# Attention pooling over 512 rows: TensorE's small matmuls and VectorE's softmax grouped for two chunks at a time

## Chip, cores and metric

One core of one Trainium2 chip. The metric is device time in microseconds, the median of three executions of the whole kernel.

## The reference

```python
h = relu(einsum('bse,eh->bsh', behavior_emb, W_b) + (candidate_emb @ W_c)[:, None, :] + fc1_b)
scores = einsum('bsh,h->bs', h, fc2_w[:, 0]) + fc2_b[0]
attn = softmax(scores, axis=-1)
user_interest = einsum('bse,bs->be', behavior_emb, attn)
x = concatenate([user_interest, candidate_emb], axis=1)
z = relu(x @ mlp1_w + mlp1_b)
logit = (z @ mlp2_w + mlp2_b)[:, 0]
```

Here B = 512 rows, S = 200 positions, E = H = 128, and everything is f32. The behavior array (52.4 MB) is read twice: once as it stands (for the pooling) and once in a copy that is transposed on the host (for the first matmul), so that some 105 MB come in.

## The kernel before, in words

**Chunks and groups.** The 512 rows are cut into 32 chunks of 16 rows. A chunk has two loads of 1.6 MB: `xt` (transposed, for the hidden layer) and `x` (as it stands, for the weighted sum). Each has four buffers. A chunk's `xt` is treated in four groups g = 0 to 3 of 800 columns (32 partial rows of 25 positions).

**What is done for a group.** The hidden layer's matmul runs as three products of rounded halves. ScalarE makes the high half (`high_half`, L329, tile `xh`), VectorE the low half (`low_half`, L454, tile `xl` = xt - xh), TensorE adds hi x hi and hi x lo (L613, L614) and, when the low half is there, lo x hi (L617) into one of three two-bank PSUM tiles `z_ps` (`products`). Bias and ReLU are taken out of PSUM by VectorE for groups 0 and 2 (`biased_max`, L464) and by ScalarE for groups 1 and 3 (`biased_relu`, L371, four instructions). Which `z_ps` a group takes is a fixed rotation (`Z_SLOTS`); TensorE waits until that tile's last group has been read.

**What is done for a chunk.** `score` (L632) is 40 column-tiled matmuls, four 32-column tiles of the array side by side, that multiply the hidden layer by fc2. VectorE's `softmax` is six small dependent steps on one chunk's scores (L475 to L493); it ends with the bias of the exponent. ScalarE's `exponents` (L336) makes the weights, GpSimd's `mask_weights` (L299) spreads them over a block-diagonal tile, and `weighted_sum` (L643) is 56 column-tiled matmuls of these weights with `x`. Every second chunk ScalarE copies the sums out (`copy_pooled4`, L342), TensorE transposes them (`transpose_sums`, L684) and ScalarE copies the result to `pooled_t` (L346).

**Order.** Each engine's order is written out by hand in a `period(c, q, phase)`, one for each chunk c, q = c mod 4 (from L381 for ScalarE, L522 for VectorE, L754 for TensorE). TensorE's is: z of groups 0 and 1 of chunk c; one column-tiled stretch with the scores of chunk c-1 and then the weighted sum of chunk c-3 (LAG = 3); z of groups 2 and 3. VectorE's is:

```python
biased_max(c, 0); low_half(c, 3); softmax(c - 1)          # six steps
next_low(0); biased_max(c, 2); next_low(1); next_low(2)   # low halves of chunk c + 1
```

and ScalarE's: ReLU of group 1; high halves 0 and 1 of chunk c+1; (copy of the sums); exponents of chunk c-1; high half 2; ReLU of group 3; high half 3.

**Loads.** SyncE issues all large loads in one queue (L252 for `xt`, L260 for `x`), in the order xt(n), x(n-3), xt(n+1), x(n-2) and so on; the last five are xt(31), x(28), x(29), x(30), x(31). xt(n) waits until the low halves of chunk n-4 are made, x(n) until chunk n-4 is summed. The weights of the last layers (`later_sb`, L266) are loaded right behind x(0).

**End.** After z of group 3 of chunk 31 TensorE goes through: row sums of the weights of chunks 0 to 27; sum of 29; scores of 31; transpose; spreading of the inverses; sum of 30; one MLP product of the candidates; the second row sums; sum of 31; the second spreading; the other candidate products (L721); transpose of the last pair; the MLP products of the pooled rows (L727) for chunks 0 to 27 and for 28 to 31; the logits (L734). VectorE adds the output bias (L589) and SyncE stores the logits in two parts (L279).

## Time and profile before

| | |
|---|---|
| median of 3 runs | 266.76 us (266.63 to 266.91) |
| the profiled execution's own time | 266.47 us |
| its span | 264.7 us |
| TensorE busy | 259.3 us (98%) |
| VectorE busy | 224.2 us (85%) |
| ScalarE busy | 200.6 us (76%) |
| GpSimd busy | 29.4 us (11%) |
| HBM read | 105.63 MB, 399 GB/s over the span |

The span is what the trace covers; the execution's own time is 1.77 us longer. TensorE's matmuls overlap and their ends are modelled, so its busy share says little; the distances between the starts of instructions are what can be added up. All times in the rows are microseconds from the span's start. "[1.05 <-DMA xt...]" at a row's end is the idle time of the engine before that instruction and what ended it.

### The profile page before, as it was taken

The page shows a single profiled execution, that of the slowest core. Times are in us where ns is not written, and L with a number is a line of the kernel's source. Part 1 is how long each engine was busy: PE and PEld are TensorE (multiplying, and loading weights), DVE is VectorE, ACT ScalarE, POOL GpSimd, SP SyncE. Part 2 cuts the span into 40 slices and gives each one's busy share as a digit, 9 for nine tenths or more (in the row PEclk, how much of TensorE's full clock was granted, in tenths as well). Part 3 has the DMA queues.
Part 4 walks back from the last instruction along what each step waited for, and adds up shares of the span by engine and source line. Part 5 has one row for each costly group of instructions (what it writes and reads, how often), then busy time and mean ns, then how long its engine had stood idle before and what let it go on. Part 6 is the DMA issues. An engine that isn't in the chain of part 4 may idle for free.

```text
span 264.7 us, 10384 instructions
## 1 busy us (share of the span) xinstructions
PE 259.3 (98%) x3942; PEld 212.4 (80%) x3942; DVE 224.2 (85%) x397; ACT 200.6 (76%) x481; POOL 29.4 (11%) x38
## 2 busy tenths in 40 slices
PE   8999999999999999999999999999999999999995
PEld 7557788888888868888888888888888888888973
DVE  0479998999898988989899998989989898999541
ACT  2569888798887697878789887878888787889312
POOL 2003001111110111110111111011111100111100
PEclk9999999999999999999999999999999999999999
DMA  7999999999999999999999999999999999999900
GB/s 247 430 433 422 422 426 420 424 424 420 426 422 423 426 420 429 429 426 426 424 429 429 426 426 426 428 428 422 428 429 428 426 426 426 429 428 426 391 32 0
DMA packets 10544, 105.87 MB, mean 400 GB/s; under 512 B 1184, under 2 KB 1696, under 8 KB 2592
## 3 DMA queue, kind: packets, MB, share of 16 engines
q1 hardware_dynamic: 10240, 105.44, 94.7%
q8 instruction: 12, 0.20, 0.3%
q10 hardware_dynamic: 288, 0.20, 0.2%
q14 instruction: 4, 0.03, 0.0%
HBM read 105.63 MB, written 0.00 MB: 399 GB/s over the span
## 4 chain that ended last, share of the span: by engine, by line
PE 60%; DMA 18%; DVE 14%; issue 4%; ACT 1%; DVEq 1%; POOL 0%; ACTq 0%; SPq 0%; POOLq 0%
DMA xt<-in_behavior_t 18%; PE s_ps L632 12%; PE u_ps L643 11%; PE z_ps L617 10%; PE z_ps L613 9%; DVE xl L454 9%; PE z_ps L614 8%; DVE hidden L464 5%; PE z_ps L608 4%; PE z_ps L750 2%; PE z_ps L643 1%; ACT xh L329 1%; PE z_ps L684 1%; PE z_ps L727 1%; PE z_ps L721 1%
## 5 line engine op out<-in xcount | busy, mean ns | idle before, releaser
L454 DVE TENSOR_TENSOR xl<-xt,xh 128x800 fp32r<-128x800 f32 x120 | 123.2, 1047 | 8.9 <-ACT xh L329 8.7
L329 ACT CAST xh<-xt 128x800 fp32r<-128x800 f32 x120 | 100.4, 862 | 34.2 <-DMA xt<-in_behavior_t 33.1
L371 ACT ACTIVATE hidden<-z_ps,bias 128x200 f32<-128x200 f32 x256 | 88.3, 428 | 7.4 <-PE z_ps L608 3.6
L613 PE MATMUL z_ps<-xh,w_hi 128*128 128x512 f32 x240 | 86.4, 360 | 0.5 <-DVE hidden L464 0.5
L614 PE MATMUL z_ps<-xh,w_lo 128*128 128x512 f32 x240 | 79.4, 345 | 0.0
L464 DVE TENSOR_TENSOR hidden<-z_ps,neg_bias 128x800 f32<-128x800 f32 x64 | 62.9, 982 | 3.3 <-PE z_ps L608 2.0
L617 PE MATMUL z_ps<-xl,w_hi 128*128 128x512 f32 x240 | 64.8, 351 | 0.9 <-DVE xl L454 0.2
L613 PEld LDWEIGHTS z_ps<-xh,w_hi 128*128 128x128 f32 x240 | 45.0, 188 | 16.3 <-issue 6.0
L299 POOL TENSOR_TENSOR weights_by_row<-weights,masks_sb 128x400 f32<-128x400 f32 x31 | 27.6, 890 | 218.3 <-ACT weights L336 177.3
L632 PE MATMUL s_ps<-hidden,f_col 128*3 128x160 f32 (+4 forms) x1280 | 50.1, 301 | 0.0
L614 PEld LDWEIGHTS z_ps<-xh,w_lo 128*128 128x128 f32 x240 | 45.1, 188 | 5.6
L643 PE MATMUL u_ps<-x,weights_by_row 128*32 128x128 f32 (+1 forms) x1680 | 46.7, 262 | 0.0
L643 PEld LDWEIGHTS u_ps<-x,weights_by_row 128*32 128x32 f32 x1680 | 42.3, 110 | 1.1
L632 PEld LDWEIGHTS s_ps<-hidden,f_col 128*3 128x3 f32 (+4 forms) x1280 | 32.3, 90 | 11.6 <-issue 4.2
L617 PEld LDWEIGHTS z_ps<-xl,w_hi 128*128 128x128 f32 x240 | 38.0, 188 | 4.1 <-DVE xl L454 4.0
L475 DVE STREAM_TRANSPOSE scores<-s_ps 128x160 f32<-128x160 f32 x32 | 10.9, 339 | 3.3 <-PE s_ps L632 3.1
L336 ACT ACTIVATE weights<-scores,exp_bias 128x25 f32<-128x25 f32 x32 | 10.9, 340 | 3.3 <-DVE exp_bias L493 3.3
L608 PE MATMUL z_ps<-xt,weights_sb 128*128 128x512 f32 (+1 forms) x32 | 11.9, 516 | 0.0
L608 PEld LDWEIGHTS z_ps<-xt,weights_sb 128*128 128x128 f32 x32 | 6.1, 199 | 5.1 <-issue 4.4
L493 DVE SCALAR_TENSOR_TENSOR exp_bias<-row_max,shift 128x1 f32<-128x1 f32 x32 | 7.0, 220 | 3.4
L483 DVE STREAM_TRANSPOSE part_max_t<-part_max 128x32 f32<-128x32 f32 x32 | 6.8, 213 | 1.1
L489 DVE STREAM_TRANSPOSE row_max<-row_max_t 128x32 f32<-128x32 f32 x32 | 6.8, 212 | 1.1
(65 smaller groups left out, 77.6 us busy)
## 6 DMA issues: line engine op xcount, KB each, us to landing
x<-in_behavior SPq DMA_DIRECT2D x32, 1600.0 KB, 26.6
xt<-in_behavior_t SPq DMA_DIRECT2D x30, 1600.0 KB, 23.7
xt<-in_behavior_t SPq DMA_DIRECT2D x4, 400.0 KB, 4.9
xt<-in_behavior_t SPq DMA_DIRECT2D x2, 800.0 KB, 7.7
later_sb<-in_later SPq DMA_DIRECT2D x1, 258.5 KB, 19.6
first_sb<-in_cand_rest SPq DMA_DIRECT2D x1, 192.0 KB, 5.7
first_sb<-in_first ACTq DMA_DIRECT2D x1, 128.0 KB, 4.8
masks_sb<-in_masks SPq DMA_DIRECT2D x1, 114.0 KB, 6.8
```

Of the source, the lines that this page charges most:

```text
L299: nc.gpsimd.tensor_tensor(weights_by_row[buf][:, :, pair_half[buf]], weights[buf][:, :].unsqueeze(2).to_broadcast([P, TILES, ROWS]), row_m ...
L329: nc.scalar.copy(xh[g][:, :], xt[q][:, g, :]).then_inc(xh_made, 1)
L336: nc.scalar.activation(weights[buf][:, :].rearrange("p (r t) -> p r t", t=RUN), score_runs(buf), ACT.Exp, bias=exp_bias[buf][:, :], accum_ ...
L371: op = nc.scalar.activation(hidden[q % 2][:, g, :, mine], z[:, :, mine], ACT.Relu, bias=bias[:, bass.ds(c * ROWS + g * EACH + b, 1)])
L454: nc.vector.tensor_tensor(xl[g][:, :], xt[q][:, g, :], xh[g][:, :].bitcast(F32), ALU.subtract).then_inc(xl_made, 1)
L464: nc.vector.tensor_tensor(hidden[q % 2][:, g, :, :].rearrange("p t (b s) -> p t b s", s=PARTS), z, nb.to_broadcast([P, TILES, EACH, PARTS] ...
L608: op = nc.tensor.matmul(z[:, a:b], w_b, xt[q][:, g, a:b], start=True, stop=True)
L613: nc.tensor.matmul(z[:, a:b], w_hi[:, :], xh[g][:, a:b], start=True, stop=False)
L614: nc.tensor.matmul(z[:, a:b], w_lo[:, :], xh[g][:, a:b], start=False, stop=False)
L617: op = nc.tensor.matmul(z[:, a:b], w_hi[:, :], xl[g][:, a:b], start=False, stop=True)
L632: op = nc.tensor.matmul(s_ps[g * Q:g * Q + rows, 0:RUN * Q].rearrange("p (t s) -> p t s", s=Q), f2_col[:, 0:rows], hidden[buf][:, g, r * R ...
L643: return nc.tensor.matmul(bank[g * Q:(g + 1) * Q, cols], weights_by_row[buf][:, t, :], x[q][:, t * E + cols.start:t * E + cols.stop], star ...
```

## The change

`LAG` goes. TensorE's column-tiled stretch is only in the periods of even chunks from 2 on, again behind group 1, and does two chunks: the weighted sums of chunks c-4 and c-3, and then the scores of chunks c-2 and c-1. Periods of odd chunks have none, except the last (31), which has the scores of 30 and the sum of 28. The two chunks' scores lie side by side in one bank, and VectorE treats both in one softmax of seven steps, placed behind low halves 2 and 3 of chunk c and 0 and 1 of chunk c+1. Hidden tiles, the `z_ps` rotation, GpSimd's waits, the order of the loads (two `xt`, then two `x`; `later` behind xt(31)), the load of x(31) (two pieces) and the order at the end follow.

```diff
-Z_SHORT = (6, 14)
+Z_SHORT = (3, 11)
 PHASE_AT = 1
 WHOLE = 2
-LAG = 3
...
-        hidden = [sb(f"hidden{i}", [P, GROUPS, TILES, Q]) for i in range(2)]
-        scores = [sb(f"scores{i}", [P, RUN * Q]) for i in range(2)]
+        hidden_first = [[sb(f"hidden_first{i}_{g}", [P, TILES, Q]) for g in range(2)] for i in range(2)]
+        hidden_rest = [sb(f"hidden_rest{i}", [P, TILES, Q]) for i in range(2 * GROUPS - 2)]
+        scores = sb("scores", [P, 2, RUN * Q])
...
-        SOFTMAX_STEPS = 6
-        FIRST = 7
+        PAIR_STEPS = 7
+        ALONE_STEPS = 6
+        FIRST = 6
         LAST = CHUNKS - 1
+        IN_PAIRS = (LAST - 1) * PAIR_STEPS
...
+        def hidden_of(q, g):
+            if q % 2 == 0 and g < 2:
+                return hidden_first[q // 2][g]
+            return hidden_rest[g - 2 if q % 2 == 0 else g + 2]
+        def hidden_free(c, q, g):
+            return c - 3 if q % 2 == 0 and g < 2 else c - 1
...
+            load_transposed(X_BUFS, 0)
             load(0, None)
+            load(1, None)
+            for c in (X_BUFS + 1, X_BUFS + 2):
+                load_transposed(c, c - X_BUFS)
+            load(2, None)
+            load(3, None)
+            with sp.Fori(0, CHUNKS // X_BUFS - 2) as turn:
+                for j in (0, 2):
+                    c = turn * X_BUFS + (2 * X_BUFS - 1 + j)
+                    load_transposed(c, (X_BUFS - 1 + j) % X_BUFS)
+                    load_transposed(c + 1, j)
+                    load(c - 3, j)
+                    load(c - 2, j + 1)
+            load_transposed(LAST, LAST % X_BUFS)
             sp.dma_start(later_sb[:, :], later).then_inc(later_loaded, 16)
-            for c in range(X_BUFS, 2 * X_BUFS):
-                load_transposed(c, c - X_BUFS)
-                load(c - LAG, None if c - LAG < X_BUFS else c - LAG - X_BUFS)
-            with sp.Fori(0, CHUNKS // X_BUFS - 2) as turn:
-                for j in range(X_BUFS):
-                    c = turn * X_BUFS + (2 * X_BUFS + j)
-                    load_transposed(c, j)
-                    load(c - LAG, (j - LAG) % X_BUFS)
-            for c in range(CHUNKS - LAG, CHUNKS):
+            for c in range(CHUNKS - X_BUFS, LAST):
                 load(c, c % X_BUFS)
+            sp.wait_ge(pooled_done, CHUNKS - X_BUFS)
+            cols = LAST_RUN * E
+            sp.dma_start(x[LAST % X_BUFS][:, 0:cols], behavior_v[LAST, :, 0:cols]).then_inc(x_half, 16)
+            sp.dma_start(x[LAST % X_BUFS][:, cols:], behavior_v[LAST, :, cols:]).then_inc(x_loaded[LAST % X_BUFS], 16)
...
+                    pool.wait_ge(xl_made, (c - buf + 3 - WHOLE) * GROUPS + (2 + buf))
...
+                    high_half(c, q, 3, None, False)
+                    biased_relu(c, q, 1, phase)
+                    exponents(c - 1, (q + 1) % 2, IN_PAIRS + 2 * ALONE_STEPS, False)
+                    biased_relu(c, q, 3, phase)
+                    return
+                if phase > 1:
+                    high_half(c, q, 3, None, phase == WHOLE)
+                if q % 2 == 1:
+                    next_half(0)
+                    biased_relu(c, q, 1, phase)
+                    next_half(1)
+                    biased_relu(c, q, 3, phase)
+                    next_half(2)
+                    return
                 biased_relu(c, q, 1, phase)
                 next_half(0)
                 next_half(1)
-                if phase == 1:
-                    exponents(0, 0, True)
-                if flush:
-                    copy_pooled4(c - LAG, u_ps)
-                if phase == 1:
-                    biased_relu(c, q, 3, phase)
-                    next_half(2)
-                else:
-                    exponents(c - 1, (q + 1) % 2, phase <= 2)
-                    next_half(2)
-                    biased_relu(c, q, 3, phase)
-                next_half(3)
+                if phase > 2:
+                    copy_pooled4(c - X_BUFS + 1, u_ps)
+                next_half(2)
+                for n in range(2):
+                    exponents(c - 2 + n, n, pair_steps(c - 2) + 2 * (PAIR_STEPS - 1 + n), phase == 2)
+                biased_relu(c, q, 3, phase)
...
+                if phase >= (X_BUFS if q % 2 == 0 and g == 0 else 2) and (q % 2 == 0 or g == 0):
+                    dve.wait_ge(scores_done, hidden_free(c, q, g))
...
+                        op = nc.vector.transpose(scores[:, :, :].rearrange("p c t -> p (c t)"), s_ps[:, 0:2 * RUN * Q])
...
+                    op = nc.vector.tensor_reduce(part_max[:, 0:n], mine, axis=AX.XY, op=ALU.max)
...
+                if step >= 5:
+                    k = step - 5
+                    own = shift[:, bass.ds(c + k, 1)]
+                    op = nc.vector.scalar_tensor_tensor(exp_bias[k if buf is None else buf][:, :], row_max[:, k:k + 1],
+                                                        own, own, ALU.add, ALU.subtract, reverse1=True)
+                op.then_inc(softmax_step, 2)
...
-                biased_max(c, q, 0, phase < 2)
-                if phase == 1:
+                biased_max(c, q, 0, phase)
+                if phase == LAST:
+                    low_half(c, q, 3)
+                    for n in range(ALONE_STEPS):
+                        softmax(c - 1, 0, n, IN_PAIRS, False)
+                    biased_max(c, q, 2, phase)
+                    return
+                if q % 2 == 1:
+                    if phase > 1:
+                        low_half(c, q, 3)
+                    next_low(0)
+                    biased_max(c, q, 2, phase)
+                    next_low(1)
+                    return
+                low_half(c, q, 2)
+                low_half(c, q, 3)
+                next_low(0)
+                next_low(1)
+                if phase == 2:
                     shifts()
                     dve.wait_ge(shift_step, 3)
-                else:
-                    if phase == 2:
-                        low_half(c, q, 2)
-                    low_half(c, q, 3)
-                for n in range(SOFTMAX_STEPS):
-                    softmax(c - 1, (q + 1) % 2, n, phase <= 2)
-                if phase == 1:
-                    biased_max(c, q, 2, True)
-                    next_low(0)
-                    next_low(1)
-                    return
-                next_low(0)
-                biased_max(c, q, 2, False)
-                next_low(1)
+                for n in range(PAIR_STEPS):
+                    softmax(c - 2, None, n, pair_steps(c - 2), phase == 2)
+                biased_max(c, q, 2, phase)
                 next_low(2)
...
+            for n in range(ALONE_STEPS):
+                softmax(LAST, 1, n, IN_PAIRS + 2 * ALONE_STEPS, False)
+            normalise(0)
+            mask_last()
             inverses(1, 1)
-            normalise(0)
             inverses(1, 2)
+            def add_out_bias(part):
+                dve.wait_ge(logit_done, part + 1)
+                nc.vector.tensor_scalar(logit[:, part, 0:quarter[part]], logit_ps[part][:, 0:quarter[part]], b_out, None,
+                                        ALU.add).then_inc(logit_made, 1)
+            add_out_bias(0)
             normalise(1)
             last_relu(0)
             last_relu(1)
-            for part in range(2):
-                dve.wait_ge(logit_done, part + 1)
-                nc.vector.tensor_scalar(logit[:, part, 0:quarter[part]], logit_ps[part][:, 0:quarter[part]], b_out, None,
-                                        ALU.add).then_inc(logit_made, 1)
+            add_out_bias(1)
...
-                    if phase == 1 and g == PHASE_AT:
-                        shift_sums()
                     if phase == 1 and g == 3:
                         pe.wait_ge(w_lo_made, 1)
                         pe.wait_ge(masks_loaded, 16)
-                    if g == PHASE_AT and phase > LAG + 1 and (q - LAG) % 2 == 0:
-                        transpose_sums(c - LAG - 1, beside_z(q, g))
-                    if g == PHASE_AT and phase >= 1:
-                        score(c - 1, (q + 1) % 2, phase == 1)
-                    if g == PHASE_AT and phase >= LAG:
-                        weighted_sum(c - LAG, (q - LAG) % X_BUFS, phase == LAG)
+                    if g != PHASE_AT or phase < 2:
+                        continue
+                    if phase == LAST:
+                        transpose_sums(LAST - X_BUFS, beside_z(q, g))
+                        score(LAST - 1, (q - 1) % X_BUFS, pair_steps(LAST - 3) + 2)
+                        weighted_sum(LAST - 3, (q - 3) % X_BUFS, False)
+                    elif q % 2 == 0:
+                        if phase == 2:
+                            shift_sums()
+                            pe.wait_ge(f2_col_made, 2)
+                        if phase == FIRST:
+                            transpose_sums(c - X_BUFS - 1, beside_z(q, g))
+                        if phase > 2:
+                            weighted_sum(c - 4, q, phase == 4)
+                            weighted_sum(c - 3, (q + 1) % X_BUFS, False)
+                        score(c - 2, (q - 2) % X_BUFS, None if phase == 2 else pair_steps(c - 4) + 2)
+                        score(c - 1, (q - 1) % X_BUFS, None)
             periods(period)(pe)
...
             row_sums(0)
             weighted_sum(LAST - 2, (LAST - 2) % X_BUFS, False)
-            score(LAST, LAST % 2, False)
+            score(LAST, LAST % X_BUFS, IN_PAIRS + 2)
             transpose_sums(LAST - 2, u_ps[:, P:P + 2 * ROWS])
             spread_inverses(0)
+            for part in range(2):
+                for m in range(2):
+                    mlp_candidates(part, m)
+            row_sums(1)
             weighted_sum_alone(LAST - 1)
-            mlp_candidates(1, 0)
-            row_sums(1)
-            weighted_sum_alone(LAST)
-            spread_inverses(1)
-            mlp_candidates(0, 0)
-            mlp_candidates(0, 1)
-            mlp_candidates(1, 1)
-            transpose_sums(LAST, last_pair_ps[:, P:P + 2 * ROWS])
             mlp_pooled(0, 0)
             mlp_pooled(0, 1)
+            spread_inverses(1)
+            weighted_sum_alone(LAST)
+            logits(0)
+            transpose_sums(LAST, last_pair_ps[:, P:P + 2 * ROWS])
             mlp_pooled(1, 0)
             mlp_pooled(1, 1)
-            logits(0)
             logits(1)
```

## Rows read from the trace of the kernel before

**Rows 1.** Page, bandwidth of the DMA in 40 slices of the span

```profile
GB/s 247 430 433 422 422 426 420 424 424 420 426 422 423 426 420 429 429 426 426 424 429 429 426 426 426 428 428 422 428 429 428 426 426 426 429 428 426 391 32 0
```

**Rows 2.** Windows, two chunks: us, busy PE, PEld, DVE, ACT, POOL, then PEclk, DMA, GB/s

```profile
215.81:231.17 15.36, 15.28 (x246) 12.83 (x242) 14.19 (x25) 12.55 (x31) 1.74 (x2) 1.00 1.01 427
```

**Rows 3.** Waits: who waited for whom, us in total, times, longest

```profile
ACT xh L329 <- DMA xt<-in_behavior_t: 33.1, 28, 2.3
```

**Rows 4.** Page, DMA issues: KB each, median us from issue to landing

```profile
xt<-in_behavior_t SPq DMA_DIRECT2D x30, 1600.0 KB, 23.7
...
later_sb<-in_later SPq DMA_DIRECT2D x1, 258.5 KB, 19.6
```

**Rows 5.** Timeline of ScalarE: start, us, instruction, idle before

```profile
215.78 1.63 ACT L329 CAST xh<-xt 128x800 fp32r<-128x800 f32 x2 [1.05 <-DMA xt<-in_behavior_t]
...
238.81 1.62 ACT L329 CAST xh<-xt 128x800 fp32r<-128x800 f32 x2 [1.48 <-DMA xt<-in_behavior_t]
```

**Rows 6.** Timeline of VectorE and GpSimd in two chunks

```profile
216.67 0.99 DVE L454 TENSOR_TENSOR xl<-xt,xh 128x800 fp32r<-128x800 f32 x1 [0.21 <-ACT xh L329]
...
217.58 0.98 DVE L464 TENSOR_TENSOR hidden<-z_ps,neg_bias 128x800 f32<-128x800 f32 x1
...
225.83 0.87 POOL L299 TENSOR_TENSOR weights_by_row<-weights,masks_sb 128x400 f32<-128x400 f32 x1 [7.00 <-ACT weights L336]
...
226.16 1.38 DVE L454 TENSOR_TENSOR xl<-xt,xh 128x800 fp32r<-128x800 f32 x1
```

**Rows 7.** Timeline of TensorE around one column-tiled stretch

```profile
212.24 0.64 PE L617 MATMUL z_ps<-xl,w_hi 128*128 128x512 f32 x2
212.71 0.30 PE L684 MATMUL z_ps<-masks_sb,pooled 128*128 128x32 f32 x2
212.94 1.56 PE L632 MATMUL s_ps<-hidden,f_col 128*32 128x160 f32 x40
214.32 1.56 PE L643 MATMUL u_ps<-x,weights_by_row 128*32 128x128 f32 x56
215.81 0.50 PE L613 MATMUL z_ps<-xh,w_hi 128*128 128x512 f32 x1
...
217.01 0.39 PE L613 MATMUL z_ps<-xh,w_hi 128*128 128x512 f32 x1
```

**Rows 8.** Timeline of VectorE: first and last step of chunk 31's softmax

```profile
251.96 0.35 DVE L475 STREAM_TRANSPOSE scores<-s_ps 128x160 f32<-128x160 f32 x1 [1.97 <-PE s_ps L632]
...
253.29 0.22 DVE L493 SCALAR_TENSOR_TENSOR exp_bias<-row_max,shift 128x1 f32<-128x1 f32 x1
```

**Rows 9.** Page, costliest groups: a transpose of 32 columns

```profile
L483 DVE STREAM_TRANSPOSE part_max_t<-part_max 128x32 f32<-128x32 f32 x32 | 6.8, 213 | 1.1
```

**Rows 10.** Timeline of all engines near the end

```profile
238.60 0.50 PE L613 MATMUL z_ps<-xh,w_hi 128*128 128x512 f32 x1
...
250.34 1.57 PE L632 MATMUL s_ps<-hidden,f_col 128*32 128x160 f32 x40
...
256.76 0.27 ACT L342 COPY pooled<-z_ps 128x128 f32<-128x128 f32 x1 [2.78 <-PE z_ps L643]
...
258.59 0.36 PE L684 MATMUL z_ps<-masks_sb,pooled 128*128 128x32 f32 x2
...
258.78 1.75 PE L727 MATMUL z_ps<-pooled_n,later_sb 128*128 128x448 f32 x4
...
259.04 0.18 ACT L346 COPY pooled_t<-z_ps 128x32 f32<-128x32 f32 x1 [2.01 <-PE z_ps L684]
...
259.33 0.22 DVE L515 TENSOR_TENSOR pooled_n<-z_ps,pooled_t 128x64 f32<-128x64 f32 x1 [3.33 <-ACT pooled_t L346]
...
260.37 0.33 PE L727 MATMUL s_ps<-pooled_n,later_sb 128*128 128x64 f32 x2
...
260.74 0.28 DVE L572 TENSOR_SCALAR z_all<-s_ps,later_sb 128x64 f32<-128x64 f32 x1 [1.19 <-PE s_ps L727]
...
262.06 1.21 SPq L279 DMA_DIRECT2D out_logit<-logit  x2
```

125 lines of the change are left out of this document (59 added, 66 removed).

## The prediction

> **What bounds the kernel now.** The page's bandwidth by slices comes first: behind the first slice it stands at 420 to 433 GB/s until the last three [rows 1], and in a window of two chunks the DMA share is 1.01 at 427 GB/s [rows 2]. The reader should see a stream that never pauses. A load lands 23.7 us after its issue, at 1600 KB / 427 GB/s = 3.84 us for each load, so about six are always under way [rows 4]: the stream isn't waiting for buffers, and two chunks (four loads) take 15.36 us whatever the engines do. The waits say the same from the other side: ScalarE waits 28 times, 33.1 us in all, for an `xt` to land [rows 3]. TensorE's busy 15.28 of 15.36 us [rows 2] counts overlapped matmuls; what matters is what lies behind each landing, and above all behind the last `xt`, that of chunk 31, which ScalarE takes up at 238.81 [rows 5]. From there to the span's end are 25.9 us of computation. So the change can gain or lose in two places: by the state in which TensorE is when xt(31) lands, and by the order of the end. It can lose in a third: if the engines' loop gets longer than 15.36 us for two chunks.
>
> **The landing of xt(31).** Four `x` loads still follow it, and the same loads precede it but one: `later` (258.5 KB [rows 4], 0.6 us at 427 GB/s) is now behind it. So xt(31) lands at 238.2, xt(29), four loads ahead, at 222.8. That the loads now come in pairs may change the stream's rate; slices differ by 1% [rows 1], which gives 1 us to either side.
>
> **TensorE's stretch.** Before, a stretch is L617 to L684 0.47 us, to the scores 0.23, scores 1.38, sum 1.49 to the next z product, whose first group then takes 1.20 [rows 7]. For two chunks I take 2 x 1.40 for the sums (the last start-to-start includes leaving the column tiles) and 1.38 + 1.49 for the scores: 5.67 us from the first sum to z of group 2. What is saved is entering and leaving once for every two chunks, some 0.3 us by these distances (bounds 0 and 0.6). It lies beside the stream and is worth nothing while the DMA sets the pace.
>
> **VectorE's order, step by step.** Here is the loss. (1) In an even chunk's period, low halves 0 and 1 of the next chunk stand ahead of the softmax, and they need that chunk's `xt`, the later of what the engine waits for. From the landing: cast at 215.78, first low half at 216.67, the next instruction 0.91 later [rows 5, 6]; so two low halves end the wait 0.9 + 2 x 0.90 = 2.7 us behind the landing, and the softmax starts there. (2) The softmax of two chunks. One chunk's goes from 251.96 to 253.29 + 0.22, 1.55 us [rows 8]. The transpose has 320 columns in place of 160: 0.35 us against 0.21 for 32 columns [rows 8, 9] makes about 0.16 more (bounds 0 and 0.35); the maximum over twice as much 0.03; the second bias with its wait 0.25. Sum 2.0, and 2.05 with the step to the next instruction. For two chunks that's 1 us less than twice one, but it now stands in one piece. (3) Behind it come, in order, bias and maximum of (c,2), low half (c+1,2), maximum (c+1,0), low halves (c+1,3) and (c+2,0), maximum (c+1,2), low half (c+2,1): seven instructions of 0.90 start to start and 0.09 for the last to end, 6.4 us [rows 6]. (4) GpSimd's spreading of the first chunk's weights, 0.87 us, starts some 0.5 us behind the exponent and overlaps the second of the seven by about 0.45. Such an overlap of 0.54 us made a low half 1.38 us where another is 0.99 [rows 6]; I charge 0.35 (bounds 0 and 0.9, as the second mask may hit another). (5) L617 of (c+2,1) starts 0.06 behind its low half, then 0.47 + 0.23 to the sums and 5.67 to z of group 2 [rows 7].
>
> On step 4 the trace shows a low half stretched by 0.39 us for 0.54 us of overlap. The Trainium skill, "SBUF — State Buffer", on the port pair that VectorE and GpSimd share, has an exclusive lock held for the whole instruction: the loser waits the overlap out. By it the term would be 0.45, and the sum 0.1 us more for each pair.
>
> Sum from the landing of xt(29): 2.7 + 2.05 + 6.4 + 0.35 + 0.06 + 0.70 + 5.67 = 17.9 us. Hence z of (30,2) starts at 222.8 + 17.9 = 240.7; before it started at 238.60 [rows 10]. That is **2.1 us later**, with the same work left: z (30,2) to (31,1), scores of 30, sum of 28, z (31,2) and (31,3), row sums, sum of 29, scores of 31. Before, this took 250.34 - 238.60 = 11.7 us [rows 10]; the scores of 31 start at 252.4.
>
> The loop closes just so: from a softmax's start, 2.05 + 6.4 + 0.35 + 0.76, then 2.8 + 1.38 to the last scores and 1.62 from their start to the next softmax (250.34 to 251.96 [rows 8, 10]) make **15.36 us, as much as the DMA's four loads**. ScalarE isn't behind: its 12.55 us of 15.36 [rows 2] stay the same work. At the start nothing is gained that lasts, since the stream is full from the second slice.
>
> **The end.** From the scores of 31 TensorE did 8.25 us without a gap of note up to 258.59 (among it the sums of 30 and 31 and all candidate products) and then 1.59 of pooled products [rows 10]. After the change both stand ahead of the end of the sum of 31: it ends at 252.4 + 9.85 = 262.25. Softmax, mask and `normalise(0)` lie under it. Then only a chain is left: ScalarE's copy, 0.2 + 0.27 + 0.05; transpose to `pooled_t` to `pooled_n`, 258.59 to 259.33 + 0.22, 1.0 with its step; pooled products 0.37 to the first ReLU, 0.22 + 0.28 for the second [rows 10]; second logits and output bias, which no row shows alone: 0.7, between 0.5 and the 1.32 from the first ReLU to the store [rows 10]. That makes 265.3 for the last store's issue. Before, it was the second of two issued from 262.06 in 1.21 us, so at 262.67, and the span ended 2.0 later. New span 267.3: 2.1 from the loop and 0.5 from the end's order. The piece-wise load of x(31) is worth nothing: it has landed long before 260.7, where its sum starts. The last slices' fall to 32 GB/s puts that near 252 [rows 1].
>
> The profiled execution is 266.47 us for a span of 264.7, so mine is 269.1; the median shown is 0.29 above, which makes 269.4. A measurement of this kernel can tell some 0.2% (0.53 us) from no change.
>
> **Rival A, the loop exceeds the DMA's pace.** Each of some twelve pairs from chunk 6 on then adds its excess. A semaphore or a mask that costs 0.2 to 0.35 us more for a pair gives 2.4 to 4.2 us: 271.8 to 273.6. For it: my loop has no slack at all, and the trace lacks the 320-column transpose. Against: sum (1) has bounds to both sides. Chance 0.25.
>
> **Rival B, TensorE sets the pace (faster).** If the low halves don't hold the softmax, TensorE is some 0.3 us a pair ahead and waits at xt(31) alone. Then z of (31,0) starts 0.9 behind 238.2, where before it started two groups (1.20 + 1.1) behind 238.60, the scores of 31 at about 248.6, and with my end the time is 1.8 - 0.5 = 1.3 below: 265.5. It decides if VectorE's seven instructions take under 4.3 us rather than 6.4. The stretches cut in half stand for it: the Trainium skill, "TensorEngine Tiling (Array Packing)", Key Properties, has every change of tiling mode drain TensorE. Here leaving shows as z's 1.20. Chance 0.10.
>
> **Rival C, no change (266.2 to 267.3).** The stream runs 1% faster with paired loads, or the low halves overlap more, and the 2.6 us are given back. The first slices of `xt` alone did run at 430 to 433 GB/s [rows 1]. Chance 0.10.
>
> **How the numbers follow.** My own case, chance 0.50: 268.2 to 270.8. With A and 0.05 for other slow cases, slower has 0.80, same 0.10, faster 0.10. The range 267.0 to 273.0 leaves out B, most of C and the far end of A.
>
> **What would show it.** Right: one softmax for two chunks of about 2.0 us that starts some 2.7 us behind the cast of an odd chunk; periods of 15.4 us for two; z of (30,2) near 240.7; the sum of 31 ending near 262; DMA at 427 GB/s as before. Wrong: VectorE idle for longer ahead of the softmax than for an `xt`, TensorE waiting for `hidden` or PSUM tiles, slices below 415 GB/s, or z of (30,2) at 238.6 or sooner.

## The result and the profile after

The changed kernel takes **283.34 us** (median of four, 282.53 to 283.6), beside 266.74 us (266.63 to 266.91) for the kernel before: a ratio of 1.0617 [1.0595, 1.0639]. The forecast was 269.4 with a range up to 273.0: the sign was right, the size wrong by a factor of six. The profiled execution took 282.53 us with a span of 280.7 (before 264.7), so 16.0 us have to be found.

The page after the change: busy time, the bandwidth of the DMA in 40 slices, one group and one kind of DMA issue (us from issue to landing last).

```profile
PE 262.6 (94%) x3942; PEld 212.8 (76%) x3942; DVE 209.3 (75%) x321; ACT 195.9 (70%) x481; POOL 28.8 (10%) x38
...
GB/s 252 434 427 429 424 424 425 422 422 429 418 425 427 425 430 419 430 427 425 430 423 430 425 423 429 425 414 425 419 410 427 378 421 425 381 90 382 7 2 3
...
L523 DVE STREAM_TRANSPOSE scores<-s_ps 128x320 f32<-128x320 f32 x15 | 7.7, 516 | 22.0 <-issue 12.4
...
xt<-in_behavior_t SPq DMA_DIRECT2D x30, 1600.0 KB, 10.6
```

VectorE does 15 us less work, as the edit intends (209.3 against 224.2 us), and that bought nothing. The stream does pause now: slices of 414, 410, 378 and 381, where [rows 1] had none under 420 between the first and the last three. A load of `xt` lands 10.6 us behind its issue instead of 23.7 [rows 4]: fewer loads are under way, the queue is waiting for buffers. The DMA no longer sets the pace.

The waits of the changed kernel (who waited for whom, us in total, times, longest). "Issue" stands for idle time for which the profile names nothing that ended it:

```profile
DVE scores L523 <- issue: 12.4, 8, 2.8
DVE scores L523 <- PE s_ps L687: 9.4, 6, 3.4
PE z_ps L670 <- DVE hidden_rest L508: 7.7, 15, 2.6
...
PE s_ps L687 <- issue: 4.2, 3, 1.7
...
ACT xh L364 <- DMA xt<-in_behavior_t: 2.8, 1, 2.8
```

The wait for `xt`, 28 times and 33.1 us in [rows 3], is down to one of 2.8 us. In its place TensorE waits once in every pair (15 times) for VectorE's `hidden_rest`, that is for a PSUM tile to be read, and VectorE waits for the scores. Three more waits, 4.2 us together, are TensorE's own inside the column-tiled stretch and are put down to "issue".

The windows show two kinds of loss. Each runs from one transpose of the sums (L741) to the next, two chunks, the third to 0.07 us behind it (us, busy PE, PEld, DVE, ACT, POOL, then PEclk, DMA, GB/s):

```profile
54.04:72.05 18.01, 15.88 (x245) 12.99 (x244) 13.06 (x20) 12.24 (x32) 1.74 (x2) 1.00 1.01 425
72.05:89.43 17.38, 15.86 (x245) 13.05 (x244) 13.10 (x20) 12.31 (x32) 1.74 (x2) 1.00 1.01 424
89.43:105.40 15.97, 15.49 (x246) 12.88 (x244) 13.14 (x20) 12.33 (x32) 1.74 (x2) 1.00 1.01 426
...
232.07:247.86 15.79, 15.47 (x244) 12.84 (x243) 13.10 (x20) 12.31 (x32) 1.74 (x2) 1.00 0.82 347
```

From 89.43 on a pair takes 15.84 us (158.43 us for ten) against 15.36 [rows 2], and by the last of them the DMA share is 0.82. The earlier pairs take 17.4 to 18.0 us. Why, TensorE's timeline of the first long stretch says:

```profile
36.59 2.95 PE L699 MATMUL u_ps<-x,weights_by_row 128*32 128x128 f32 x112
...
40.17 0.43 PE L687 MATMUL s_ps<-hidden_first,f_col 128*2 128x160 f32 x2
41.96 0.30 PE L687 MATMUL s_ps<-hidden_first,f_col 128*2 128x160 f32 x1 [1.36 <-issue]
...
43.97 0.50 PE L670 MATMUL z_ps<-xh,w_hi 128*128 128x512 f32 x1
```

In the middle of the scores TensorE stands still, and no instruction that it could be waiting for ends there: from one row of the timeline to the next 1.79 us, where such steps are otherwise 0.14. The same happens at 60.02 and 77.75 and never again. The stretch from the first sum to the next z product takes 7.38, 7.74 and 7.21 us these three times and 5.60 us all eleven later times: 5.5 us lost.

The steady loop, all engines, from the end of a stretch:

```profile
232.07 0.30 PE L741 MATMUL z_ps<-masks_sb,pooled 128*128 128x32 f32 x2
232.31 2.95 PE L699 MATMUL u_ps<-x,weights_by_row 128*32 128x128 f32 x112
...
235.08 0.31 PE L687 MATMUL s_ps<-hidden_first,f_col 128*32 128x160 f32 x2
...
237.91 0.50 PE L670 MATMUL z_ps<-xh,w_hi 128*128 128x512 f32 x1
...
238.10 0.52 DVE L523 STREAM_TRANSPOSE scores<-s_ps 128x320 f32<-128x320 f32 x1 [1.09 <-issue]
...
240.64 0.99 DVE L508 TENSOR_TENSOR hidden_rest<-z_ps,neg_bias 128x800 f32<-128x800 f32 x1
...
241.03 0.87 POOL L335 TENSOR_TENSOR weights_by_row<-weights,masks_sb 128x400 f32<-128x400 f32 x1 [13.04 <-ACT weights L371]
...
241.55 1.20 DVE L498 TENSOR_TENSOR xl<-xt,xh 128x800 fp32r<-128x800 f32 x1
...
241.77 0.49 PE L670 MATMUL z_ps<-xh,w_hi 128*128 128x512 f32 x1 [0.32 <-DVE hidden_rest L508]
...
243.79 1.41 ACT L408 ACTIVATE hidden_rest<-z_ps,bias 128x200 f32<-128x200 f32 x4
...
245.25 0.50 PE L670 MATMUL z_ps<-xh,w_hi 128*128 128x512 f32 x1
...
246.36 0.98 DVE L498 TENSOR_TENSOR xl<-xt,xh 128x800 fp32r<-128x800 f32 x1
...
247.39 0.63 PE L674 MATMUL z_ps<-xl,w_hi 128*128 128x512 f32 x2
...
247.86 0.30 PE L741 MATMUL z_ps<-masks_sb,pooled 128*128 128x32 f32 x2
```

This is the ring, and it is the prediction's: from L741 6.03 us to the softmax, 2.54 for the softmax, then VectorE's seven instructions back to back from 240.64 to 247.34 (6.70), L674 0.05 behind the last of them, L741 0.47 further on: **15.79 us**, which is the window. Every other pair takes some 0.12 us more, and 15.84 is the mean. A second path runs beside it: z (c,2) is read only at 240.64, z (c+1,1) needs that PSUM tile and starts at 241.77 in place of 237.91 + 1.20 + 2 x 1.09 = 241.29. It is the wait that the profile lists, 7.7 us in all. It doesn't set the pace: from 241.77 to L741 are 6.09 us, and five groups at TensorE's own distances (1.18 + 3 x 1.09 + 0.73 + 0.36) are an estimated 5.5, so this path has some 0.5 us to spare. A third one, through ScalarE, whose ReLU ends at 245.20 just ahead of z (c+2,0) at 245.25, has an estimated 0.3 (245.25 + 1.18 + 0.73 + 0.36 against 247.86). All three hang on the same thing, a softmax that starts when the scores end, last in the stretch, and takes 2.54 us in one piece. And the end:

```profile
253.69 0.50 PE L670 MATMUL z_ps<-xh,w_hi 128*128 128x512 f32 x1
...
265.97 1.57 PE L687 MATMUL s_ps<-hidden_rest,f_col 128*32 128x160 f32 x40
...
274.08 1.60 PE L699 MATMUL z_ps<-x,weights_by_row 128*32 128x128 f32 x56
```

**The bill.** z (30,2) starts at 253.69 against 238.60 [rows 10], 15.1 us later; from there to the span's end it takes 27.0 us against 26.1.

| where | us |
|---|---|
| z (4,2) at 43.97 against 38.52: 5.45, less the 1.78 of the first stall | 3.7 |
| three stalls inside stretches: 1.78 + 2.14 + 1.61 | 5.5 |
| the other loss in 13 pairs (209.72 against 200.08 us, less 2.14 + 1.61) | 5.9 |
| from z (30,2) to the end | 0.9 |
| sum | 16.0 |

### The profile page after: what moved, and what is told of

It is laid out like the page before. It is cut to its first block, busy times and chain, and to the rows that moved or that the text cites. A ratio compares the mean times of both kernels' runs of the same rounds, so it can differ in the third digit from the quotient of the medians.

```text
span 280.7 us, 10369 instructions
## 1 busy us (share of the span) xinstructions
PE 262.6 (94%) x3942; PEld 212.8 (76%) x3942; DVE 209.3 (75%) x321; ACT 195.9 (70%) x481; POOL 28.8 (10%) x38
## 4 chain that ended last, share of the span: by engine, by line
PE 64%; DVE 16%; issue 10%; DMA 4%; ACT 2%; DVEq 1%; SPq 1%; ACTq 0%
PE u_ps L699 15%; PE z_ps L670 13%; PE s_ps L687 12%; PE z_ps L674 10%; PE z_ps L671 9%; DVE hidden_rest L508 5%; DMA xt<-in_behavior_t 4%; DVE scores L523 3%; DVE exp_bias L544 2%; DVE part_max L531 1%; DVE part_max_t L533 1%; DVE row_max L539 1%; PE z_ps L699 1%; ACT xh L364 1%; DVE row_max_t L535 1%
## 5 line engine op out<-in xcount | busy, mean ns | idle before, releaser
L498 DVE TENSOR_TENSOR xl<-xt,xh 128x800 fp32r<-128x800 f32 x120 | 118.7, 1019 | 16.2 <-ACT xh L364 15.9
L408 ACT ACTIVATE hidden_rest<-z_ps,bias 128x200 f32<-128x200 f32 x192 | 67.0, 449 | 3.0 <-PE z_ps L665 1.7
L674 PE MATMUL z_ps<-xl,w_hi 128*128 128x512 f32 x240 | 64.9, 351 | 0.0
L508 DVE TENSOR_TENSOR hidden_rest<-z_ps,neg_bias 128x800 f32<-128x800 f32 x48 | 47.2, 983 | 3.5 <-PE z_ps L665 2.0
L687 PE MATMUL s_ps<-hidden_rest,f_col 128*4 128x160 f32 (+4 forms) x960 | 47.2, 299 | 1.7 <-issue 1.7
L674 PEld LDWEIGHTS z_ps<-xl,w_hi 128*128 128x128 f32 x240 | 37.9, 188 | 1.3
L687 PEld LDWEIGHTS s_ps<-hidden_rest,f_col 128*4 128x4 f32 (+4 forms) x960 | 33.3, 90 | 5.8 <-issue 2.1
L687 PE MATMUL s_ps<-hidden_first,f_col 128*2 128x160 f32 (+4 forms) x320 | 25.5, 299 | 2.5 <-issue 2.5
L523 DVE STREAM_TRANSPOSE scores<-s_ps 128x320 f32<-128x320 f32 x15 | 7.7, 516 | 22.0 <-issue 12.4
L408 ACT ACTIVATE hidden_first<-z_ps,bias 128x200 f32<-128x200 f32 x64 | 23.4, 515 | 0.7 <-PE z_ps L665 0.7
L687 PEld LDWEIGHTS s_ps<-hidden_first,f_col 128*32 128x32 f32 (+4 forms) x320 | 15.4, 90 | 6.7 <-issue 3.2
L508 DVE TENSOR_TENSOR hidden_first<-z_ps,neg_bias 128x800 f32<-128x800 f32 x16 | 15.7, 979 | 0.0
## 6 DMA issues: line engine op xcount, KB each, us to landing
xt<-in_behavior_t SPq DMA_DIRECT2D x30, 1600.0 KB, 10.6
```

What stands on the lines that cost most here:

```text
L408: op = nc.scalar.activation(hidden_of(q, g)[:, :, mine], z[:, :, mine], ACT.Relu, bias=bias[:, bass.ds(c * ROWS + g * EACH + b, 1)])
L498: nc.vector.tensor_tensor(xl[g][:, :], xt[q][:, g, :], xh[g][:, :].bitcast(F32), ALU.subtract).then_inc(xl_made, 1)
L508: nc.vector.tensor_tensor(hidden_of(q, g)[:, :, :].rearrange("p t (b s) -> p t b s", s=PARTS), z, nb.to_broadcast([P, TILES, EACH, PARTS]) ...
L523: op = nc.vector.transpose(scores[:, :, :].rearrange("p c t -> p (c t)"), s_ps[:, 0:2 * RUN * Q])
L674: op = nc.tensor.matmul(z[:, a:b], w_hi[:, :], xl[g][:, a:b], start=False, stop=True)
L687: op = nc.tensor.matmul(s_ps[g * Q:g * Q + rows, q % 2 * RUN * Q:(q % 2 + 1) * RUN * Q] .rearrange("p (t s) -> p t s", s=Q), f2_col[:, 0:r ...
```

## The experiments

All times stand beside runs of the kernel before on the same chip (medians 266.46 to 266.85 us). Where no range is given the kernel ran once. Theory P puts the loop's loss down to the order inside the stretch (scores last), S to the raise of the softmax's semaphore by 2, F puts the stalls down to the supply of TensorE's instructions.

**e1_inc1: the softmax steps raise their semaphore by 1.**

```diff
-                op.then_inc(softmax_step, 2)
+                op.then_inc(softmax_step, last + 2 if step == last else 1)
```

> The changed kernel, but VectorE's softmax steps raise their semaphore by 1 (the last by what is left) in place of 2. Theory S (the raise by 2 makes each dependent step some 0.08 us later): steps of 0.22 to 0.25 us apart in chunk 31's softmax as before the change, the pair's softmax 0.4 to 0.5 us shorter, the two-chunk period 15.4 in place of 15.8, 4 to 6 us less in all: 277 to 279. Rival (the steps are longer by the pair's layout or by register work): the same distances as in the changed kernel, 283.

Measured: 278.34 us (277.62 to 279.99), 5.0 less than the change; ratio to before 1.0461 [1.0419, 1.0503]. A pair takes 15.52 us (139.7 for nine). The softmax goes from 219.10 to 221.41, 2.31 where the change has 2.59 in such a pair, and 2.25 for 2.54 in the others; it also starts 0.06 earlier behind L742 (L741 of the change). The three stalls are all there (stretches of 7.64, 7.73, 7.48). So S is real: the step distances are worth 0.32 us a pair and 4.2 of the 5.0 us. The last pair's softmax stands behind the loop, in code that runs once:

```profile
250.07 0.52 DVE L523 STREAM_TRANSPOSE scores<-s_ps 128x320 f32<-128x320 f32 x1 [1.09 <-PE s_ps L688]
...
252.08 0.98 DVE L508 TENSOR_TENSOR hidden_rest<-z_ps,neg_bias 128x800 f32<-128x800 f32 x1
```

It takes 2.01 us, and so, within 0.01, do those of the first two pairs (at 27.18 and 44.31, written out ahead of the loop). In the loop it takes 0.24 to 0.30 us more, all of it around the biases of the exponent.

**e2_split: the two sums behind group 0, the two scores behind group 1.**

```diff
+                    if g == 0 and phase > 2 and phase != LAST and q % 2 == 0:
+                        weighted_sum(c - 4, q, phase == 4)
+                        weighted_sum(c - 3, (q + 1) % X_BUFS, False)
```

> The changed kernel, but the two weighted sums stand behind group 0 of the even chunk and the two scores behind group 1, so that the stretch is two halves of 112 and 80 matmuls with one z product between. Theory F (TensorE's instructions come too slowly when 192 small matmuls, 384 instructions, run one behind the other the first time and the load queue is full): the three stretches of 7.2 to 7.7 us at 36, 54 and 72 us shrink by most of their 1.6 to 2.1 us of stall, 3 to 5 us less in all, with 0.3 us a pair for entering and leaving twice where TensorE is on the path: 279 to 283. Rival D (those stretches wait for data): the stalls stay, 283 to 286.

Measured: 295.48 us, a miss for both. The stalls shrink to 0.35 + 1.10 + 0.71 us (the scores' part is 3.20, 3.95, 3.56 and then 2.85), but a pair takes 17.2 us. The waits say why:

```profile
DVE xl L498 <- ACT xh L364: 51.7, 16, 3.5
ACT pooled_t L381 <- PE z_ps L741: 32.0, 14, 2.5
...
PE z_ps L670 <- DVE hidden_rest L508: 22.5, 15, 2.5
```

ScalarE has the copy of the transposed sums ahead of its ReLU of group 1 and of the next high halves, VectorE's low halves wait for these, and the softmax stands behind the low halves. By these waits a move of TensorE's work alone shifts the ring to ScalarE.

**e3_half_after and e4_half_before: no loads of `x` for chunks 4 to 31**, in the changed kernel and in the one before.

```diff
-                    load(c - 3, j)
-                    load(c - 2, j + 1)
```

> The changed kernel without the x loads of chunks 4 to 31 (their weighted sums use the x of chunks 0 to 3), so that the load queue is half as full. Theory F: no stall in the stretches at 36 to 77 us, 5 to 6 us less. Theory P (the two-chunk period of 15.8 is set by the engines: scores, softmax, reading of z group 2, which frees the PSUM tile that the next chunk's group 1 needs): the period stays at 15.7 to 15.8, the end 250 + 20 us: 274 to 278 in all. Rival (the DMA still sets the pace): the period falls below 15.5.

> The kernel before without the x loads of chunks 4 to 31. If its period of 15.36 us for two chunks is the DMA's, it falls to TensorE's own 14.9 to 15.1 and the whole to 257 to 262; if the engines set it, it stays at 266.

Measured: 282.06 and 261.96 us. Windows of two chunks, first of the changed kernel, then of the one before:

```profile
200.20:216.00 15.80, 15.50 (x246) 12.84 (x245) 13.11 (x20) 12.33 (x31) 1.74 (x2) 1.00 0.57 210
```

```profile
193.70:208.80 15.10, 15.10 (x244) 12.82 (x243) 13.77 (x25) 13.03 (x31) 1.75 (x2) 1.00 0.61 220
```

With the DMA half idle the changed loop is as long as ever (15.84), and the loop of before gets shorter, 15.1 in place of 15.36. So the engines bound the one and the DMA the other, and the engines of before had only 0.26 us of slack a pair. The stalls: the third shrank (stretch 6.38), the first two stayed (7.70, 7.65). The loads that are left fall into just these two stretches: the DMA share is 1.05 from 36.80 to 40.40 and 1.07 from 54.80 to 58.50, although the whole window from 54.8 to 72.7 moves only 210 GB/s. So these two say nothing against a part of the traffic; in the third it is 0.90.

**e5_peeled: four more periods written out ahead of the loop**, two of which have a long stretch.

```diff
-                for c in range(FIRST):
-                    body(c, c % X_BUFS, c)
+                for c in range(FIRST + X_BUFS):
+                    body(c, c % X_BUFS, min(c, FIRST))
```

> The changed kernel with four more periods (chunks 6 to 9) written out ahead of the loop, so that TensorE's instructions are new up to chunk 13 rather than 9; the work is the same. Theory F (the stalls need instructions that run for the first time while the load queue is full): stalls of 1.5 to 2 us in the stretches of chunks 10 and 12 too (near 90 and 106 us), 3 to 4 us more in all, 286 to 287. Rival (the stalls belong to the time of the run, while the load queue holds most, not to the code): stalls in the same three stretches as before this edit, 283.

Measured: 286.81 us. Five stretches stall instead of three: 7.24, 7.38, 7.67, 7.67 and 7.59 us, then 5.60 from 126.0 on. The waits of this kernel:

```profile
PEld s_ps L687 <- issue: 9.4, 5, 2.1
```

and the packets of the DMA queue that the page calls "instruction" (packets, MB, share), first of the change, then of this kernel:

```profile
q8 instruction: 12, 0.20, 0.3%
```

```profile
q8 instruction: 16, 0.26, 0.4%
```

This decides for new code: two stretches are added that have not been run yet, and just two more stall, at 90.2 and 108.2, where the change (at 89.7 and 105.6) runs at 5.60. The same work in later passes through the loop does not.

**e8_scores_first: the scores in front of the sums**, otherwise as the change.

```diff
+                        score(c - 2, (q - 2) % X_BUFS, None if phase == 2 else pair_steps(c - 4) + 2)
+                        score(c - 1, (q - 1) % X_BUFS, None)
                         if phase > 2:
                             weighted_sum(c - 4, q, phase == 4)
                             weighted_sum(c - 3, (q + 1) % X_BUFS, False)
-                        score(c - 2, (q - 2) % X_BUFS, None if phase == 2 else pair_steps(c - 4) + 2)
-                        score(c - 1, (q - 1) % X_BUFS, None)
```

> The changed kernel with the two scores in front of the two weighted sums in the stretch. Theory P (VectorE's softmax, and the reading of z group 2 behind it, wait for the scores, which come last in the stretch): the softmax starts some 1 to 1.5 us earlier from the stretch's start, VectorE's idle time ahead of it goes, and the two-chunk period falls from 15.8 to the DMA's 15.4: 5 to 6 us less, 277 to 278. Rival (the period is set by VectorE's or ScalarE's seven to nine instructions, not by when the scores come): 15.8 as before this edit; or the scores wait for ScalarE's last ReLU and the gain is lost.

Measured: 275.07 us, 8.3 less than the change, and 15.22 us a pair (137.0 for nine). Its loop, all engines:

```profile
229.62 0.51 DVE L523 STREAM_TRANSPOSE scores<-s_ps 128x320 f32<-128x320 f32 x1
...
230.36 0.50 PE L670 MATMUL z_ps<-xh,w_hi 128*128 128x512 f32 x1
...
232.14 0.99 DVE L508 TENSOR_TENSOR hidden_rest<-z_ps,neg_bias 128x800 f32<-128x800 f32 x1
```

The softmax is as long as in the change (2.52), but it starts right behind its two low halves, 0.74 us ahead of z (c,2) rather than 0.19 behind, z (c,2) is read 1.78 us behind its start, not 2.73, and VectorE has gaps again. That is 0.62 us a pair less (15.84 - 15.22): P is shown. By the waits (TensorE 14 times for ScalarE's ReLU, 5.2 us) the new ring goes through ScalarE, and at 15.22 us it is shorter than the DMA's 15.36. It can run below that only while loads have landed ahead of their use: the DMA share is 1.01 from 102.60 to 117.90, and behind the start nothing waits for a load. One stretch more now stalls, chunk 30's at 239.9 (7.02 us), whose code stands behind the loop and is new too. In the change that one, at 248.1, had its 5.60; what differs is told under e13.

**e9_inc1_first: both edits.**

> Both: softmax steps raise the semaphore by 1, and scores stand in front of the sums. If P and S hold, TensorE alone sets the pace between the landings: period at the DMA's 15.36, and the time lost in the three stalls is partly won back: 269 to 274. If the two gains are the same one, 277.

Measured: 274.58 us (274.38 to 274.62), ratio 1.0298 [1.0282, 1.0314]. Also 15.22 us a pair, so S adds nothing to P in the loop: once the softmax is off the path, its length costs nothing. Four stretches stall (7.22, 7.43, 7.30 and 7.43 us for the one of chunk 30), 7.0 us in all. z (4,2) starts at 43.3 against 38.52, and 5.4 us of stalls follow; less 13 x 0.14 for the shorter period that makes z (30,2) some 8.3 us late (it is 7.9, at 246.5), and the span is 8.1 us longer. So what's left to a pair version is its start and its stalls, and a loop that is 1% ahead of the DMA can't win them back.

**e10_before_inc2: the kernel before, its softmax steps raised by 2.**

```diff
-                op.then_inc(softmax_step, 1)
+                op.then_inc(softmax_step, 2)
```

> The kernel before with one edit: its six softmax steps raise their semaphore by 2. Theory S: the distances of chunk 31's steps grow from 0.22 to 0.25 to about 0.30 to 0.33, and VectorE's softmax by 0.4 us a chunk; as VectorE has 1.2 us to spare in two chunks and the stream sets the pace, the whole changes by 0 to 1 us: 266.7 to 267.7. Rival (the step's price belongs to the pair's kernel): distances unchanged.

Measured: 266.5 us, ratio 0.9999 [0.999, 1.0008]. VectorE in chunk 31's softmax, which answers to [rows 8]:

```profile
252.08 0.35 DVE L475 STREAM_TRANSPOSE scores<-s_ps 128x160 f32<-128x160 f32 x1 [2.03 <-PE s_ps L632]
...
253.75 0.22 DVE L493 SCALAR_TENSOR_TENSOR exp_bias<-row_max,shift 128x1 f32<-128x1 f32 x1
```

First to last start is 1.67 us in place of 1.33, with durations unchanged: five distances, 0.07 us each. In the loop four of the five grow by that much; the one ahead of the bias is 0.34 either way. The price is there on its own, and it costs nothing where the chain isn't on the path.

**e11_three_one: e9 with the second sum behind z of group 2**, so that no stretch holds over 136 matmuls, and ScalarE's copy of the sums last in its period.

```diff
+                    if g == 2 and 2 < phase < LAST and q % 2 == 0:
+                        weighted_sum(c - 3, (q + 1) % X_BUFS, False)
```

> The changed kernel with steps that raise by 1, scores in front, and the second chunk's weighted sum moved behind z group 2, so that the long stretch has 136 matmuls in place of 192 and ScalarE's copy of the sums comes last. Theory F: the stalls of the first passes fall from some 1.7 us each to under 0.6, 4 us less than with the whole stretch (274.6), if the period stays at 15.2 to 15.4: 270 to 272. Rival (a stretch of 136 stalls as much, since what counts is the queue of loads): 274 to 276.

Measured: 274.73 us (274.25 to 275.23), ratio 1.03 [1.0283, 1.0316]. The long stretches run at 4.22 us from the first on, but the first two stalls have only moved into z of group 2 behind them:

```profile
42.54 0.39 PE L672 MATMUL z_ps<-xh,w_lo 128*128 128x512 f32 x1 [1.04 <-issue]
...
59.60 0.40 PE L675 MATMUL z_ps<-xl,w_hi 128*128 128x288 f32 x1 [0.74 <-issue]
```

From that z to the sum behind it are 2.49 and 2.30 us where later pairs have 1.30, and the third pair's sum takes 1.91 for 1.51: 2.6 us in all, where the same three pairs lost 5.2 in e9. So about half of F's part held. And a pair takes 16.6 us twice, 15.9 once and then 15.53 (155.3 for ten), because ScalarE now waits for its ReLU of group 3:

```profile
ACT xh L364 <- PE z_ps L675: 29.2, 15, 3.2
...
ACT hidden_rest L408 <- PE z_ps L675: 15.9, 15, 1.6
```

The total was missed: what the smaller stalls gave, the longer ring took.

**e12_before_end: the kernel before with the changed order at the end.**

```diff
-            weighted_sum_alone(LAST - 1)
-            mlp_candidates(1, 0)
-            row_sums(1)
-            weighted_sum_alone(LAST)
...
+            for part in range(2):
+                for m in range(2):
+                    mlp_candidates(part, m)
+            row_sums(1)
+            weighted_sum_alone(LAST - 1)
...
+            weighted_sum_alone(LAST)
+            logits(0)
```

> The kernel before with the changed kernel's order at the end (candidate products ahead, pooled products of the first 28 chunks ahead of the sum of 31, first logits ahead of the last transpose). By the prediction's term the end is 0.5 us longer, 267.2. Rival: TensorE's own gaps are filled and the end is shorter, 266.3 or less.

Measured: 267.18 us (266.74 to 267.41), ratio 1.0025 [1.0016, 1.0034], 0.7 us over its neighbour's 266.46.

**e13_two_x: `x` of chunks 0 and 1 alone is loaded**, so that the traffic is down before the second stall.

> The changed kernel with the x loads of chunks 0 and 1 alone (all weighted sums use these two), so that the load queue is short from some 30 us on, 6.4 MB less ahead of it than in the run without the x loads from chunk 4. Theory F (new instructions reach TensorE late because the queue of loads is full): the stretches of chunks 6 and 8 (near 54 and 71 us) take 5.6 us in place of 7.2 to 7.7, that of chunk 4 (at 36) at most half its stall; 277 to 279 in all. Rival (the first pass through 384 instructions stalls whatever the loads do): three stalls of 1.6 to 2.1 us and 282 to 283.

Measured: 282.24 us; stretches of 6.74, 7.37, 6.40, then 5.60. Windows around the second one, at 55.1:

```profile
44.00:54.00 10.00, 9.75 (x70) 7.46 (x63) 8.12 (x14) 7.45 (x20) 1.74 (x2) 1.00 0.39 134
54.00:58.00 4.00, 4.00 (x124) 3.81 (x126) 3.17 (x5) 4.00 (x10) 0.00 (x0) 1.00 0.81 339
58.00:62.00 4.00, 2.65 (x78) 2.02 (x74) 1.81 (x2) 0.81 (x2) 0.00 (x0) 1.00 0.94 327
```

The stalls shrink by 0.6, 0.4 and 0.8 us and stay: the total was missed. But the pair of `xt` loads falls into the stretch itself, so the DMA is busy just then (0.94) although it idles around it. The run alone doesn't separate the two.

**What the packets of all runs say of the stalls.** The traces hold each DMA packet's time. On queue 8 ("instruction") every packet has 16,384 bytes. In the change seven come up to 81.6 us, none from there to 249.1, and five to the end: they come with code that runs for the first time. One comes in every stalled stretch, and TensorE goes on a fixed while behind its end:

| stretch | packet starts, behind the stretch's start | packet ends | TensorE goes on |
|---|---|---|---|
| change, 36.59 | 3.01 | 40.61 | 41.96 |
| change, 54.27 | 3.32 | 58.66 | 60.02 |
| change, 72.28 | 2.95 | 76.33 | 77.75 |
| e8, 239.92 | 3.29 | 244.30 | 245.67 |
| change, 248.09 (no stall) | 1.00 | 250.28 | |

The same holds for all 29 stalls that the profiles of e1, e2, e3, e5, e8, e9, e11, e13 and the change list for TensorE's matmuls: each ends 1.2 to 1.6 us behind the end of such a packet. So F is shown: TensorE waits for its code. The last two rows are the same code behind the loop with another order of its halves. From the stretch's start to the packet the windows are, in the change and in e8:

```profile
248.09:249.10 1.01, 1.01 (x45) 1.01 (x48) 1.01 (x3) 1.01 (x4) 0.00 (x0) 1.00 0.07 16
```

```profile
239.92:243.20 3.28, 3.28 (x109) 2.77 (x112) 2.18 (x4) 3.28 (x9) 0.00 (x0) 1.00 0.93 394
```

With the DMA free (0.07) the packet starts 1.0 us into the stretch (1.5 in e1). With loads under way (0.93, and 0.97 in e9) it starts some 2.3 us later, e8 against the change and e9 against e1, and the stretch stalls. When a packet was asked for no trace shows, so that the traffic delays it is inferred from these pairs.

**e6_before_later: the kernel before, with only the later weights moved** behind xt(31), as the change has them.

```diff
-            sp.dma_start(later_sb[:, :], later).then_inc(later_loaded, 16)
             for c in range(X_BUFS, 2 * X_BUFS):
...
+            sp.dma_start(later_sb[:, :], later).then_inc(later_loaded, 16)
             for c in range(CHUNKS - LAG, CHUNKS):
                 load(c, c % X_BUFS)
```

> The kernel before with one edit: the last layers' weights (258.5 KB) are loaded behind the last transposed chunk rather than behind x(0). As the last transposed load then lands 0.6 us earlier and the stream sets the pace, 0.4 to 0.6 us less than before: 266.1 to 266.3. Rival (something else than that landing bounds the end): no change, 266.7.

Measured: 265.77 us (265.73 to 265.91), ratio 0.997 [0.9958, 0.9981]. It is the fastest kernel of the study that makes all its loads, 0.8 us below the kernel before.

## Why the prediction was wrong, point by point

**The whole miss.** The forecast's span was 267.3 us, the measured one 280.7. Of these 13.4 us, 13.0 lie ahead of z (30,2), which was forecast at 240.7 and starts at 253.69: 5.9 of the loop, 3.7 of the start and 5.5 of the stalls, less the 2.1 that the forecast had. Three steps failed: the softmax's term was 0.49 us too small, and the start and TensorE's first passes were put at nothing.

**What bounds the kernel: right for before.** The DMA did set the pace (e4). The sentence that the change can lose "if the engines' loop gets longer than 15.36 us" named the place, and my sum put the loop at 15.36 with no slack. Measured 15.84: rival A, at more than its 0.2 to 0.35 us a pair. A sum that comes out at the DMA's pace to the hundredth says that any error to one side counts 13 times and to the other side not at all; the forecast took it as no loss.

**TensorE's stretch: right.** 5.67 us forecast, 5.60 measured once the code has run. Leaving and entering once less saves 0.14 us inside the stretches (2 x 2.87 - 5.60); with some 0.1 each for L617 ahead of a stretch (0.47 for 0.36) and for z's first group behind it (1.20 for 1.09) that is an estimated 0.35, near the forecast 0.3. What it lacks is the first pass through the code, 7.2 to 7.7 us; no row of before could show that, as its own first stretches (at 28.19 and 35.65) take the usual 2.87.

**Steps 1 and 2, the softmax.** It starts 6.03 us behind L741 as the ring's terms say (2.8 + 1.38 + 1.62 and 0.23), though TensorE's scores are what it waits for and not the low halves of step 1. The transpose of 320 columns takes 516 ns, the forecast 0.51. But the whole takes 2.54 us for 2.05, and **this is the term that failed**: "The softmax of two chunks" took its distances from [rows 8], where each step raises its semaphore by 1. The diff shows the 2; I read it as bookkeeping and gave it no line. By e1 it is worth 0.28 us of the softmax. The other part is a wrong row: chunk 31's softmax is code that runs once, and there the forecast was right, 2.01 us by e1. In the loop the kernel before already had longer steps around the bias, 0.34 us where [rows 8]'s softmax has 0.25:

```profile
223.37 0.21 DVE L489 STREAM_TRANSPOSE row_max<-row_max_t 128x32 f32<-128x32 f32 x1
223.71 0.22 DVE L493 SCALAR_TENSOR_TENSOR exp_bias<-row_max,shift 128x1 f32<-128x1 f32 x1
```

In e1's loop that makes 2.25 to 2.31, some 0.27 more. The sum with 2.54 in place of 2.05 is 15.85, and 15.84 was measured: an error of 0.49 us, thirteen times.

**Step 3: right.** Seven instructions of 6.4 and a mask of 0.35 were forecast, 6.70 us measured for both. What the prediction left out is the wait for the PSUM tile: the changed rotation and the tiles' readers had no line either. Nor do they set the pace; but by the trace a shorter queue on VectorE alone would have gained no more than an estimated 0.3 us a pair, until ScalarE's ReLU (ahead of z (c+2,0) at 245.25) holds the loop.

**Step 4, the mask beside a low half.** A low half is 1.20 us for 0.98, so 0.22 us for 0.35 us of overlap (241.55 to 241.90); I charged 0.35 and nothing hangs on it. The Trainium skill, "SBUF — State Buffer", has the loser wait the overlap out, which would be 0.35 here. Both traces show some 0.14 less, 0.22 for 0.35 here and 0.39 for 0.54 in [rows 6]; beyond that first 0.14 us they agree with it.

**"At the start nothing is gained that lasts": the wrong question.** What is *lost* there lasts. 3.7 us go before z (4,2): z (3,1) waits 2.55 us at 30.27 for the tile behind the first pair's softmax, and the first pair needs both its chunks. No run tried the start alone. Then the stalls of 5.5 us, which no row of before shows and no step of the prediction held. A loop with 0.14 us of slack a pair (e8) can't repay 9 us in 13 pairs, and the changed one has none.

**The end: right.** From the scores of 31 to the end of their sum 9.71 us measured (265.97 to 274.08 + 1.60) and 9.85 forecast, and 5.0 from there to the span's end, as forecast. The order's +0.5 is +0.7 by e12. The part from z (30,2) to the scores of 31 is 12.3 us for 11.7; z (31,1) waits 0.44 us for its PSUM tile there. The move of the later weights is worth 0.8 us (e6), forecast 0.6.

**Rivals B and C** are out: TensorE's saving of some 0.35 us a pair never shows, since it isn't what the loop waits for. The Trainium skill, "TensorEngine Tiling (Array Packing)", Key Properties, has every change of mode drain TensorE; here one entry and one exit less are worth no more than that estimated 0.35, 0.14 of it inside the stretches.

## What to carry to other kernels

If two steps are merged on one engine, the merged block has to start as early as it can in the stretch that feeds it: here a softmax of 2.5 us behind the last matmul of a stretch set the loop, and the same block started 0.9 us earlier, beside the sums, left the path. A loop whose slack is under 2% turns every loss at the start into a loss at the end, so look at the first passes on their own: long runs of short matmuls are dearest where their code is new, and writing a loop out makes more of it. And test a change's parts alone: the one part worth having was a small load moved behind the last one that matters.

## What the runs showed of the hardware that was not expected

- TensorE can run out of code. In a run of 192 short column-tiled matmuls (each with its weight load) that is executed for the first time it stops for 0.8 to 2.1 us in the middle, and goes on 1.2 to 1.6 us behind the end of a 16,384-byte packet on the queue "instruction" (29 stalls in nine runs). Written out five times, the run stops five times (e5). 96 in a row, as in the kernel before, never show it; with 112 and 80 and one z group between it is 2.2 us in three passes for 5.5 (e2), and with 136 it moves into the z group behind, 2.6 us for 5.2 (e11). New code doesn't stall when the packet comes early, 1.0 to 1.5 us into the stretch, as it does with few loads under way (chunk 30 in the change, e1, e3, e5 and e13); it does when loads run at full rate (chunk 30 in e8 and e9).
- Raising a semaphore by 2 instead of 1 on VectorE lengthens a dependent step by 0.07 us (e10), with the instruction's own duration unchanged. In the loop the step to the bias, 0.34 us long, doesn't grow (e1, e10).
- The same six VectorE steps take longer inside a loop than written out: the step to the bias 0.34 us for 0.25 in the kernel before, and a pair's softmax 2.25 to 2.31 for 2.01 in e1. What the loop does there no trace shows.
